# A recommendation tower on one core: gathers joined into one table, eight tables picked, pair sums moved by DMA

## The reference

```python
e = jnp.stack([tbl_0[ids[:, 0]], ..., tbl_25[ids[:, 25]]], axis=1)
sd = jnp.einsum('bfd,bd->bf', e, dense)
ss = jnp.einsum('bfd,bgd->bfg', e, e)
z = jnp.concatenate([dense, sd, ss[:, iu, ju]], axis=1)   # iu, ju: upper triangle, 325 pairs
h = jnp.concatenate([z, dense], axis=1)                   # 607 features
h = jnp.maximum(h @ W_top1 + b_top1, 0.0)                 # 512
h = jnp.maximum(h @ W_top2 + b_top2, 0.0)                 # 256
y = h @ W_top3
```

## Time and profile before

| What | us |
|---|---|
| median of 3 runs (lowest to highest) | 134.25 (133.89 to 136.73) |
| the profiled execution | 133.41 |
| its span, first to last instruction | 131.6 |

### The profile page before, as it was taken

How to read it: one execution, slowest core, us unless ns; L and a number is a source line. 1 busy time by engine, 2 the same in 40 slices (tenths; PEclk the granted TensorE clock), 3 DMA queues, 4 the chain that set the end, 5 groups by cost and what they waited for, 6 DMA issues and landing times.

```text
span 131.6 us, 2179 instructions
## 1 busy us (share of the span) xinstructions
PE 108.2 (82%) x752; PEld 95.4 (72%) x752; DVE 80.3 (61%) x217; ACT 87.6 (67%) x240; POOL 79.2 (60%) x87
## 2 busy tenths in 40 slices
PE   0649999999399978499897869987897998784992
PEld 0346668685288968499796869977887997783991
DVE  4399979899480099923639980447994063997011
ACT  5379989999238299991539997327999342997101
POOL 4778788787878777777787787777777800000000
PEclk9999999999999999999999999999999999999999
DMA  3998675379822122122122121221221200000000
GB/s 66 298 224 145 176 209 138 97 240 412 295 57 62 41 61 60 40 65 57 42 60 50 50 65 40 60 62 42 62 59 41 65 22 0 0 0 0 5 0 1
DMA packets 4803, 11.42 MB, mean 87 GB/s; under 512 B 2244, under 2 KB 2244, under 8 KB 4664
## 3 DMA queue, kind: packets, MB, share of 16 engines
q0 software_dynamic: 2560, 5.25, 15.7%
q1 hardware_dynamic: 2232, 6.03, 15.3%
HBM read 11.27 MB, written 0.00 MB: 86 GB/s over the span
## 4 chain that ended last, share of the span: by engine, by line
PE 38%; ACT 21%; POOL 15%; DVE 10%; issue 7%; DMA 7%; ACTq 0%
PE ps_h_bank L378 17%; POOL rows L265 15%; ACT dots L613 13%; PE ps_gram L360 6%; PE ps_gram L291 6%; PE ps_gram L390 5%; DMA rows<-in_tbl,ids_sb 5%; ACT dots L617 4%; DVE dots L501 4%; ACT dots L610 3%; DVE vecs L474 2%; PE ps_dve L322 2%; DVE dots L505 1%; DMA ids_sb<-in_ids 1%; PE ps_act L322 1%
## 5 line engine op out<-in xcount | busy, mean ns | idle before, releaser
L265 POOL DMA_INDIRECT rows<-in_tbl,ids_sb x80 | 78.4, 980 | 25.5 <-issue 23.5
L360 PE MATMUL ps_gram<-vecs 128*128 128x104 f32 x256 | 31.3, 277 | 6.9 <-ACT dots L617 5.0
L360 PEld LDWEIGHTS ps_gram<-vecs 128*128 128x128 f32 x256 | 29.5, 192 | 8.9 <-DVE dots L505 6.2
L378 PE MATMUL ps_h_bank<-dots,w_dots 128*128 128x128 f32 x192 | 22.4, 277 | 5.5 <-ACT dots L617 3.7
L378 PEld LDWEIGHTS ps_h_bank<-dots,w_dots 128*128 128x128 f32 x192 | 21.7, 192 | 6.2 <-DVE dots L505 6.2
L613 ACT COPY dots<-ps_gram 32x48 f32<-32x48 f32 x96 | 23.1, 241 | 1.3
L501 DVE COPY dots<-ps_gram 32x48 f32<-32x48 f32 x96 | 23.0, 240 | 1.6
L455 DVE TENSOR_TENSOR one_hot<-ps_gram,row_id 125x1024 fp32r<-125x1024 f32 (+1 forms) x18 | 19.1, 1095 | 3.5 <-PE ps_h_bank L279 3.5
L291 PE MATMUL ps_gram<-one_hot,table_hi 125*128 125x512 f32 x48 | 20.6, 450 | 0.0
L542 ACT COPY vecs<-ps_act 128x512 f32<-128x512 f32 (+1 forms) x12 | 10.4, 871 | 13.8 <-PE ps_act L322 13.7
L291 PE MATMUL ps_gram<-one_hot,table_lo 125*128 125x512 f32 x48 | 19.5, 428 | 0.0
(11 more groups left out here) (41 smaller groups left out, 96.4 us busy)
## 6 DMA issues: line engine op xcount, KB each, us to landing
table<-in_tbl SPq DMA_DIRECT2D x6, 448.0 KB
w_dots<-in_w_dots SPq DMA_DIRECT2D x1, 1536.0 KB, 7.5
rows<-in_tbl,ids_sb POOLq DMA_INDIRECT x80, 2.5
w_dense<-in_w_dense SPq DMA_DIRECT2D x1, 512.0 KB, 3.7
w<-in_W_top SPq DMA_DIRECT2D x1, 512.0 KB
table<-in_tbl SPq DMA_DIRECT2D x6, 52.0 KB
dense<-in_r_dense_features SPq DMA_DIRECT2D x1, 256.0 KB, 5.8
ids_sb<-in_ids SPq DMA_DIRECT2D x1, 52.0 KB, 1.8
```

The source lines that it names most:

```text
L265: pool.indirect_dma_start(out=rows[:, slot - EARLY, :], out_offset=None, in_=ins[f"tbl_{f}"], in_offset=bass.IndirectOffsetOnAxis(ap=ids[: ...
L360: last = pe.matmul(ps_gram[:, part % 2 * BANKS + g // PER_BANK, c0:c0 + COLS], vecs[:, p0:p0 + QUADS, :], vecs[:, p0:p0 + QUADS, 1:SLOTS], ...
L378: last = pe.matmul(bank[:, o, :], w1_dots[:, j, (o0 + o) * P:(o0 + o + 1) * P], dots[:, j, :], start=False, stop=(j == STEPS - 1), skip_gr ...
```

## The change

Four parts of the program differ.

1. **Gathers.** The 18 tables that stay cold are joined into one table, `cold`, on the way in. A gather still brings 128 rows of 512 B, but 16 of the 18 now bring 16 slots (tables) of 8 samples, and two bring 2 slots of 64 samples. Row numbers are the ids plus each table's place in `cold`, added by one VectorE operation. `rows` and `vecs` exist twice. After a transpose 16 slots of a sample lie side by side, so an eviction copies runs of 16 elements; parts of the gram follow the batches, part p needing the batches up to p+1, and the last part is in two halves.
2. **Picks.** Eight tables are picked in place of six, the two new ones with 10 steps. `table` is a ring of three, `table_hi` and `table_lo` are rings of 20 steps, the one-hots a ring of 24. `read_picked` writes the first two tiles' columns straight to `vecs`; `early` and `place_early` serve tiles 2 and 3 alone.
3. **Pair sums.** The gram has all 27 columns a sample. Two copies per engine and part (`read_sums`) bring the diagonal blocks, 27 partitions by 216 elements, to `sums`. Nine DMAs (`strip`, `move_strips`), each of 2 to 26 rows of 1536 B, bring a tile's `sums` to `dots`, where pairs fill 3 steps of 128 partitions, so layer 1 is 3 matmuls for each output block. SyncE issues them for tiles 0 to 2; for tile 3 SyncE, ScalarE and GpSimd issue three each.
4. **Order.** All engines' orders are written anew: gram parts of the next tile stand before layer 1 of a tile. Layers 2 and 3 use free columns of `ps_h_bank`. The weights of layer 1 are 3 steps, not 6.

Cut to its core (empty lines left out):

```diff
-HOT = [5, 6, 7, 16, 19, 24]
+TABLE_ROWS = [125000, 12500, 1250, 1250, 12500, 1000, 1000, 1000, 1250, 12500, 12500, 1250, 12500,
+              12500, 1250, 12500, 1000, 1250, 12500, 1000, 1250, 1250, 1250, 1250, 1000, 1250]
+HOT = [5, 6, 7, 16, 19, 24, 2, 3]
 NHOT = len(HOT)
-KT = 8
-KP = HOT_ROWS // KT
-KP_A = KP // 16 * 16
+KP = 125
+KP_A = 112
+KTS = [TABLE_ROWS[f] // KP for f in HOT]
+KT_MAX = max(KTS)
+STEP_COUNTS = sorted(set(KTS))
+ROW_ID_AT = [sum(n for n in STEP_COUNTS if n < kt) for kt in KTS]
...
-RING = 3
-TABLE_RING = 4
+RUNS_DVE = [[(0, 2), (2, 4)] + [(k, min(k + 2, KTS[i])) for k in range(max(KS_ACT[i]) + 1, KTS[i], 2)]
+            for i in range(NHOT)]
+STEP_AT = [sum(KTS[:i]) for i in range(NHOT)]
+HOT_STEPS, PART_STEPS, TABLE_RING = 24, 20, 3
...
-BATCHES, _slot = [], EARLY
-for _n in [len(COLD) - 4 * 4 - 1, 4, 4, 4, 4, 1]:
-    BATCHES.append((_slot, _n))
-    _slot += _n
-assert _slot == SLOTS
+COLD_AT = [sum(TABLE_ROWS[f] for f in COLD[:k]) for k in range(len(COLD))]
...
+MAIN = 16
+EXTRA_WIDTHS = [w for w in (4, 2, 1) if (len(COLD) - MAIN) & w]
+EXTRA_AT = [MAIN + sum(EXTRA_WIDTHS[:n]) for n in range(len(EXTRA_WIDTHS))]
+GATHERS = [(EXTRA_AT[n], w, p) for n, w in enumerate(EXTRA_WIDTHS) for p in range(0, P, P // w)]
+GATHERS += [(0, MAIN, p) for p in range(0, P, P // MAIN)]
+NG, NX = len(GATHERS), len(COLD) - MAIN
+assert NX <= 4 and NG == len(COLD)
+BATCHES = [(0, NX), (NX, NX + 4), (NX + 4, NX + 8), (NX + 8, NX + 12), (NX + 12, NX + 14), (NX + 14, NX + 16)]
...
+CHUNKS = PARTS + 1
+STEPS = 3
+STRIPS = SLOTS // STEPS
+STRIP_ROWS = [2, 5, 8, 11, 14, 18, 20, 24, 26]
+STRIP_AT = [sum(STRIP_ROWS[:q]) for q in range(STRIPS)]
...
+        early = sb("early", [P, EARLY, (TILES - DIRECT) * P])
+        vecs = sb("vecs", [P, 2, P, PITCH])
+        dots = sb("dots", [P, TILES, PARTS, STEPS, PITCH])
...
+        table = sb("table", [P, TABLE_RING, KT_MAX, D])
+        table_hi = sb("table_hi", [P, PART_STEPS, D], F32R)
+        table_lo = sb("table_lo", [P, PART_STEPS, D], F32R)
+        row_id = sb("row_id", [P, sum(STEP_COUNTS)])
+        minus_row_id = sb("minus_row_id", [P, sum(STEP_COUNTS)])
         distance = sb("distance", [P, max(len(ks) for ks in KS_ACT), BATCH])
-        one_hot = sb("one_hot", [P, RING, KT, BATCH], F32R)
+        one_hot = sb("one_hot", [P, HOT_STEPS, BATCH], F32R)
...
+        def picked_before(step, ring):
+            return 0 if step < ring else 1 + max(i for i in range(NHOT) if STEP_AT[i] <= step - ring)
...
+        def evictions(t, g):
+            n0, n1 = BATCHES[g]
+            bank = ps_dve if g % 2 == 0 else ps_act
+            first = [n for n in range(n0, n1) if n == n0 or GATHERS[n][0] != GATHERS[n - 1][0]]
+            for a, b in zip(first, first[1:] + [n1]):
+                slot, w, p0 = GATHERS[a]
+                yield (vecs[:, t % 2, p0:p0 + (b - a) * (P // w), EARLY + slot:EARLY + slot + w],
+                       bank[:, a - n0:b - n0, :].rearrange("d n (p f) -> d (n p) f", f=w))
+        def own_sums(t, part, s, half=None):
+            g0, n = (0, PER_PART) if half is None else (half * PER_BANK, PER_BANK)
+            b0 = part % 2 * BANKS + (half or 0)
+            src = ps_gram[PITCH * s:PITCH * s + SLOTS, b0:b0 + n // PER_BANK, :].rearrange(
+                "a k (g c) -> a (k g) c", g=PER_BANK)[:, :, SLOTS * s:SLOTS * (s + 1)]
+            return (sums[t % 2][:, :, part, :, g0:g0 + n, s], src.rearrange("a g (q j) -> a q j g", q=STRIPS))
+        def strip(t, q):
+            n = STRIP_ROWS[q]
+            return (dots[STRIP_AT[q]:STRIP_AT[q] + n, t].rearrange("p h j m -> p (h j m)"),
+                    sums[t % 2][0:n, q].rearrange("a h j g s -> a (h j g s)"))
...
+            def move_strips(t, strips):
+                sp.wait_ge(s_sums_dve, chunks_to(t, PARTS - 1))
+                sp.wait_ge(s_sums_act, chunks_to(t, PARTS - 1))
+                for q in strips:
+                    dst, src = strip(t, q)
+                    sp.dma_start(dst, src).then_inc(s_dots[t], 16)
...
+            sp.dma_start(w1_dots[:, :, :], ins["w1_dots"]).then_inc(s_w, 16)
+            sp.dma_start(w2[:, :, :], ins["W_top2"]).then_inc(s_w, 16)
+            move_strips(0, range(STRIPS))
+            move_strips(1, range(STRIPS))
+            move_strips(2, range(STRIPS))
+            move_strips(3, range(0, STRIPS, 3))
...
+            pool.wait_ge(s_cold_rows, 1)
             for t in range(TILES):
-                for g, (s0, n) in enumerate(BATCHES):
-                    if t >= 1:
-                        pool.wait_ge(s_tp, (t - 1) * NB + g + 1)
-                    for slot in range(s0, s0 + n):
-                        f = SLOT_TABLES[slot - 1]
+                for g, (n0, n1) in enumerate(BATCHES):
+                    if t >= ROW_SETS:
+                        pool.wait_ge(s_tp, (t - ROW_SETS) * NB + g + 1)
+                    for n in range(n0, n1):
                         pool.indirect_dma_start(
-                            out=rows[:, slot - EARLY, :], out_offset=None, in_=ins[f"tbl_{f}"],
-                            in_offset=bass.IndirectOffsetOnAxis(ap=ids[:, t, f:f + 1], axis=0),
-                        ).then_inc(s_rows[g], 16)
+                            out=rows[:, t % ROW_SETS, n, :], out_offset=None, in_=ins["cold"],
+                            in_offset=bass.IndirectOffsetOnAxis(ap=cold_rows[:, t, n:n + 1], axis=0),
+                        ).then_inc(s_rows[t % ROW_SETS][g], 16)
+            t = TILES - 1
+            pool.wait_ge(s_sums_dve, chunks_to(t, PARTS - 1))
+            pool.wait_ge(s_sums_act, chunks_to(t, PARTS - 1))
+            for q in range(2, STRIPS, 3):
+                dst, src = strip(t, q)
+                pool.dma_start(dst, src).then_inc(s_dots_pool, 16)
...
+            def gram(t, part, half=None):
+                if part == 0:
+                    if t < DIRECT:
                         pe.wait_ge(s_pick_read, NHOT)
-                    if part >= 2:
-                        pe.wait_ge(s_fold_dve, t * PARTS + (part - 1))
-                        pe.wait_ge(s_fold_act, t * PARTS + (part - 1))
-                    for g in range(BANKS * PER_BANK):
-                        p0 = QUADS * (part * BANKS * PER_BANK + g)
-                        c0 = g % PER_BANK * COLS
-                        last = pe.matmul(ps_gram[:, part % 2 * BANKS + g // PER_BANK, c0:c0 + COLS],
-                                         vecs[:, p0:p0 + QUADS, :], vecs[:, p0:p0 + QUADS, 1:SLOTS],
-                                         start=True, stop=True)
-                    last.then_inc(s_gram, 1)
-                dense_part(t, ps_h_act, OC1 // 2, s_h_act_read)
-                if not first:
-                    pe.wait_ge(s_fold_dve, t * PARTS + (PARTS - 1))
-                    pe.wait_ge(s_fold_act, t * PARTS + (PARTS - 1))
-                    layer_3(t - 1)
-                next_transposes(0, 1)
-                pe.wait_ge(s_fold_dve, t * PARTS + PARTS)
-                pe.wait_ge(s_fold_act, t * PARTS + PARTS)
+                    else:
+                        pe.wait_ge(s_early, t - DIRECT + 1)
+                    pe.wait_ge(s_dve_read, uses_to(t, 0))
+                g = 1 + part + (half or 0)
+                pe.wait_ge(s_dve_read if g % 2 == 0 else s_act_read, uses_to(t, g))
+                n = t * PARTS + part - 2
+                if n >= 0 and not half:
+                    pe.wait_ge(s_sums_dve, chunks_to(n // PARTS, n % PARTS))
+                    pe.wait_ge(s_sums_act, chunks_to(n // PARTS, n % PARTS))
+                for g in range(PER_PART) if half is None else range(half * PER_BANK, (half + 1) * PER_BANK):
+                    p0 = QUADS * (part * PER_PART + g)
+                    c0 = g % PER_BANK * P
+                    last = pe.matmul(ps_gram[:, part % 2 * BANKS + g // PER_BANK, c0:c0 + COLS],
+                                     vecs[:, t % 2, p0:p0 + QUADS, :], vecs[:, t % 2, p0:p0 + QUADS, 0:SLOTS],
+                                     start=True, stop=True)
+                last.then_inc(s_gram, 1)
...
+            def layer_1(t):
+                if t == 0:
+                    pe.wait_ge(s_w, 32)
+                if t < TILES - 1:
+                    pe.wait_ge(s_dots[t], 16 * STRIPS)
+                else:
+                    pe.wait_ge(s_dots[t], 16 * (STRIPS - STRIPS // 3))
+                    pe.wait_ge(s_dots_pool, 16 * (STRIPS // 3))
...
+            pick(0)
+            pick(1)
+            transposes(0, 0)
+            pick(2)
+            transposes(0, 1)
+            pick(3)
+            transposes(0, 2)
+            pick(4)
+            transposes(0, 3)
+            pick(5)
+            transposes(0, 4)
+            transposes(0, 5)
+            pick(6)
+            transposes(1, 0)
+            pick(7)
             pe.wait_ge(s_pad, 2)
-            pe.wait_ge(s_w1, 48)
-            pe.wait_ge(s_w2, 48)
-            pe.wait_ge(s_w1_fold, 1)
-            dense_part(0, ps_h_dve, 0, s_h_dve_read)
```

(80 more changed lines are left out.)

556 lines of the change are left out of this document (302 added, 254 removed).

## The result

The changed kernel takes 146.7 us (median of four runs, 144.97 to 149.11) where the kernel before took 134.45 beside it (133.89 to 136.73). The ratio is 1.079, 95% interval 1.071 to 1.087: slower, and 7 us above the top of the range. Executions of either kernel fall into a fast and a slow state, and every ratio here compares the fast ones alone, so it is not the quotient of two medians. The profiled execution took 144.97 us, its span is 143.1.

The account below looks back on a forecast made before the run. TensorE was taken to set the end, with pick-stage copies and GpSimd also checked. First gram 54.8 + work 54.5 + waits 9.7 = 119.0, with the tail 132.4; (132.4 + 1.8) × 1.006 = 135.0 us, whole range 130.0 to 139.5.

Parts of the forecast that it names:

- walk it in order: Pick stage: summing laps, transposes, handoffs and waits from pick 0's end at 17.4 puts the first gram at 54.8 us.
- Rival D: Pick stage: `table_hi`'s ring makes ScalarE and TensorE take turns; last four laps lose 3.5 us, total 138.5; chance 0.14.
- Loss of 10.9: Pick stage: eight picked tables move the first gram from 43.85 to 54.8 us, a loss of 10.9 us.
- the hop: Strip DMAs moving pair sums to `dots`: 2.1 us wait in tile 2, 4.3 us in tile 3, otherwise hidden.
- The five short waits: Tiles 2 and 3: TensorE waits for copies before gram parts and the dense part, 0.9 to 1.5 us each.
- the slope: Strided copies out of the gram and in `place_early`: 0.0019 us an element, so 0.56 us for 216 elements.
- rival B: Tiles and tail: copies at the contiguous rate, GpSimd's DMAs at SyncE's price; saves 3.8 us, total 131.3; chance 0.25.
- wait before layer 1 of tile 2: Tile 2: last strip lands at 101.5 us, TensorE has work to 99.4, so it waits 2.1 us.
- the price of a strip: Pair sums: SyncE issues each strip in 0.47 us, taken from the earlier trace.
- the last hop: Tail, tile 3's strips: 2.8 us for SyncE and ScalarE, 2.8 to 5.0 for GpSimd; 4.3 taken.
- The fixed 2.0 us: Tail: the skill's fixed cost for each DMA; with 2.0 for 1.8 the sum would be 132.8 us.
- rival C: Before tile 3's layer 1: about 5 us idle drops TensorE to 1.2 GHz, costing 2.9 us, total 137.9; chance 0.16.

Follow-up runs that it names:

- experiment 1: Changed kernel with TensorE's two transposes of tile 1's first batches (1, 0) moved behind pick 7: 139.27 us, ratio 1.044 to the kernel before.
- experiment 9: experiment 5 with tile 3's work reordered and its strips split SyncE three, ScalarE two, GpSimd four, without filler matmuls: 130.55 us, ratio 0.970 to the kernel before.
- experiment 8: experiment 1 with six picked tables instead of eight, 80 gathers and room for four in `table`: 134.75 us.
- experiment 10: experiment 1 with tile 2's nine strips read from DRAM, not from pair sums in SBUF, so its pair terms are left out: span 133.4 us.
- experiment 2: Changed kernel with 14 extra matmuls filling TensorE's stall before the transposes (1, 0) and pick 7: span 142.6 us.
- experiment 3: Changed kernel with extra matmuls filling TensorE's gaps before layer 1 of tiles 2 and 3 and the last two half gram parts: 139.91 us.
- experiment 4: Changed kernel with tile 2's nine strips issued by SyncE (five) and GpSimd (four) instead of SyncE alone: 141.45 us.
- experiment 5: Changed kernel with the edits of experiment 1 and experiment 4 together: 135.41 us.

## Why the prediction was wrong

**The pick stage: a wait was missed.** The step "walk it in order" counted 18 transposes as 2.0 us of work and never asked what releases each. The two of tile 1 are the only ones whose bank is freed by a copy that stands behind the next table's one-hots on VectorE. The prediction even had VectorE's time for those one-hots, and did not lay it beside TensorE's next instruction. In its own numbers those one-hots are out at 52.2 us, while pick 7 is to start at 53.6 − 4.6 = 49.0. It cost 6.5 us (experiment 1), 2.7 of them through the clock.

The rest of the walk came out: from the end of pick 0 to the first gram it has 37.4 us, and with the order mended it takes 37.5 to 37.7. Within it shorter waits (0.67 and 0.87 for 0.9 and 1.0, and 0.83 for the 1.2 of the last read) make up for longer laps (4.66 for 4.5, 4.75 for 4.6). Rival D did not happen: ScalarE did stand at the ring of `table_hi`, 0.47 us before rounding table 2 (3.51 in experiment 9), but TensorE had pick 1 to do. "Loss of 10.9" against six tables is 11.4 by experiment 8, right for what it named. What the walk started from was not right: pick 0 ended at 13.3 us and not at 17.4. The prediction had no reason for these 4.1 us, which hid that much of its miss.

**The tiles: the work was right, the hop was not.** Predicted 77.6, measured 85.7. The five short waits were put at 0.9, 1.0, 0.9, 1.5, 1.1 and are 0.87, 1.09, 0.71, 1.41, 0.99. The copies:

```profile
L566 DVE COPY sums_even<-ps_gram 27x216 f32<-27x216 f32 x12 | 6.5, 541 | 16.9 <-PE ps_gram L365 16.8
...
L645 ACT COPY vecs<-ps_act 128x512 f32<-128x512 f32 x8 | 5.0, 622 | 5.5 <-PE ps_act L344 5.4
L652 ACT COPY vecs<-early 128x1152 f32<-128x1152 f32 x2 | 4.4, 2215 | 0.0
```

0.54 for 0.56, 0.62 for 0.60 (1.10 before), 2.2 for 2.2: the slope held (1.8 ns an element between the two new forms, 1.9 taken), and rival B's contiguous rate did not. The gathers ended at 95.8 + 0.94 and nothing waited for their rows (the prediction had the last one out at 94.6). Two slips of its arithmetic, (104.3 + 0.94 − 2.8) / 80, which is 1.28 and not 1.27, and 256 × 0.117, which is 29.95 and not 29.8, change little. The 8.1 us that are over:

| term | predicted | measured | over |
|---|---|---|---|
| wait before layer 1 of tile 2 | 2.1 | 4.62 | 2.5 |
| that layer (2.8) and the transposes behind it (0.43) | 3.2 | 6.35 | 3.1 |
| last half gram part | 1.14 | 1.84 | 0.7 |
| sums and hop of tile 3 | 5.2 | 5.35 | 0.2 |
| layer 1 of tile 3 | 2.8 | 4.50 | 1.7 |

These come to 8.2. The first is the price of a strip, a term of the sum that was sized too small: 0.47 us came from the earlier trace rows, whose sources are in DRAM; 9 × (0.76 − 0.47) = 2.6. A strip holds SyncE for 0.72 to 0.76, and experiment 10 shows that its source makes the difference. Layer 1 of tile 0, which was to have 3 us to spare, waited 0.26 (0.89 in experiment 2). The prediction bounded GpSimd's plain DMAs from both sides, having no row, but took SyncE's for known, though no row of before moved data within SBUF. GpSimd's were then the cheapest (0.54), and ScalarE's, taken as SyncE's, the dearest (0.84, one 1.47); so the sum of the last hop came out right by luck. The Trainium skill, DMA: Bandwidth & Descriptors, section on the issuing engine by pattern, calls the path of SyncE and ScalarE generally faster; in issue time of such moves GpSimd was the faster here (0.52 to 0.56 us a strip, against 0.65 to 0.79 on SyncE). The fixed 2.0 us that the prediction quotes from the Trainium skill, DMA: Bandwidth & Descriptors, section on the anatomy of one DMA, stands there for GpSimd's path; GpSimd's strips took 1.7 to 2.0 us from issue to landing.

Rows two, three and five of the table are rival C. The mechanism was there, with 0.16, for one place and one gap of 5 us. It foresaw 2.9 us for layer 1 of tile 3 and what follows, at 0.08 a matmul; the layer alone cost 1.7 to 2.7 by run, 0.11 a matmul where all of it was slow. What was missed is that two more gaps would open, 3.41 us in the pick stage and 4.62 before tile 2, so that it struck four times, the last half gram part included: 7.0 us by experiments 2 and 3. The Trainium skill, TensorE: Matmul & The Clock Gate, part 1, says that an idle array returns to 1.2 GHz; the rows behind the waits of 3.41, 4.62 and 5.35 us agree. The prediction held that against one gap, with a small chance, where each wait of the sum should have been held against it. Two of its own signs of being wrong came: the first gram after 57 (57.36), and over 3.5 us for the last layer 1 (4.50).

So the forecast of 135.0 needed both. With the order mended and the clock held up in the tiles, the stages of experiments 1 and 3 add up to 13.6 + 37.5 + 81.4 = 132.5 us, an estimate, since no run has both edits. It would have met the 132.4 predicted by luck: 3.8 too few in the tiles, mostly the strips, against a start 3.8 shorter than assumed.

## What to carry to other kernels

When an order is written by hand, walk it instruction by instruction, and for each ask which engine frees its buffer and what stands ahead of that release there. Take a DMA's price from a row with the same kinds of source and target, and divide moves over queues by each queue's own price. Add to every new gap on TensorE the slow work behind it: mending a wait of 3.1 us gave back 5.5 in experiment 4, and one of 2.3 us gave 3.7 between experiments 1 and 5.
